# Graph attention on one core: GpSimd's two gathers of a pair also wait for VectorE's product of the pair four places back

## The chip, the cores and the metric

The kernel runs on one core of one Trainium2 chip. The metric is the device time of one execution in microseconds (us), of which the median of several executions counts. The engines are TensorE (PE; PEld is its weight load), VectorE (DVE), ScalarE (ACT), GpSimd (POOL) and SyncE (SP).

## The reference

One layer of graph attention with 8 heads, residual, a norm over the nodes and a norm over the features, all in fp32:

```python
Q, K, V = x @ Wq, x @ Wk, x @ Wv            # 6250 x 512, seen as 8 heads of 64
score = exp(clip(sum_d(K[src] * Q[dst]) / 8, -5, 5))      # 106250 edges x 8 heads
h = x + segment_sum(V[src] * score, dst) / (segment_sum(score, dst) + 1e-6)
h = (h - mean(h, 0)) * rsqrt(var(h, 0) + 1e-5) * gamma + beta
out = layernorm(x + h)                      # over the 512 features
```

The edges are sorted by `dst`.

## The kernel before

There are three stages. **project** (up to about 452 us of the profile) makes Q, K and V of 49 tiles of 128 nodes and stores K and V side by side in the HBM table `kv_d`, one row of 1024 fp32 numbers for each node. **attend** (about 452 to 1970 us) is the edge stage. **normalise** does the rest.

The edge stage works on 440 *pairs* of edge blocks; a block is up to 128 edges, one on each partition. A pair `q` has slot `s = q % 8` (`RING = 8`) of the buffer `kv`, which has 8 slots. Each engine has its own loop over the pairs, and `step(q, s, fills)` is one turn of it; `fills` counts how often the slot has been filled. What happens to pair q:

- GpSimd (`gather`, L747) issues two indirect DMAs of 128 rows x 4 KB each that fetch K and V rows of the edges' sources into `kv[:, s, u, 0:1024]`. They signal `s_g[s]`. `index` (L739) copies the row numbers of four pairs at a time.
- TensorE (L914) makes `q_ps`, the Q rows of the edges' destinations, from a one-hot matrix `mm_sb` and the Q rows of a node tile (`q_tile`). There is one `q_ps`: the step for pair q+1 waits until VectorE has used that of pair q (`s_mul`).
- VectorE multiplies K by `q_ps` in place (L794, *the product*, signals `s_mul[s]`), sums each head (L801), clips (L788).
- ScalarE takes the exponential (L855, signals `s_exp`) and weighs four heads of V with it (L841). VectorE weighs three heads (L710) and GpSimd one (L710, the same helper `weigh`). All three signal `s_v`.
- TensorE adds the weighed V rows to the node sums `acc` (L937, waits for `s_v`, signals `s_seg[s]`). It does so two steps behind, that is, after `q_ps` of the pair three on.
- GpSimd may gather the pair q+8 into the slot as soon as `s_seg[s]` says that pair q has been added up.

GpSimd's step is written in this order (`POOL_LAG = 5`): two gathers of pair q, at every fourth pair `index`, then the weighing of pair q-5. Its program has no other work in this stage. The engines' queues are worked in order, so whatever stands behind a wait waits too. SP loads a `q_tile` of 512 KB for each of the 49 node tiles.

`wait_apart(eng, sem, value)` waits for a semaphore's value; with a value in a register it makes the register, waits for 1 and then for the register's value. `at(s, fills, -4)` gives the slot and the count of the pair four back.

Of the kernel before, what the change touches and what calls it, by code (L numbers as in the profile page):

```python
# [44 lines left out]
RING = 8  # L45
# [29 lines left out]
def wait(eng, sem, value):  # L75

    if not (isinstance(value, int) and value <= 0):
        eng.wait_ge(sem, value)


def wait_apart(eng, sem, value):


    if not isinstance(value, int):
        value = eng.snap(eng.to_reg(value))
        eng.wait_ge(sem, 1)
    wait(eng, sem, value)
# [538 lines left out]
def attend(nc, block, kv_d, q_d, lb_d, nb_d, xb_d, tabs, agg, rz, kv, first, x_first, s_first, s_slots, soft):  # L626
    lb, nb, q_tile, zeros, less, eps = first
    src_t, bits_row, cnt_row, ident = tabs
    with ExitStack() as ctx:
# [9 lines left out]
        def sems(name):  # L639
            return [sem(f"{name}{s}") for s in range(RING)]  # L640
# [11 lines left out]
        s_mul, s_red, s_clip, s_exp = sems("s_mul"), sems("s_red"), sems("s_clip"), sems("s_exp")  # L652
# [6 lines left out]
        s_qx, s_evc, s_evict = (soft[n] for n in ("s_qx", "s_evc", "s_evict"))  # L659
        s_rz = soft["s_rz_early"]  # L660
        POOL_LAG = 5
        LOOKAHEAD, LAG = 3, 3

        def pipeline(eng, step, head):
# [9 lines left out]
        def there(q):  # L674
            return not isinstance(q, int) or 0 <= q < PAIRS

        def at(s, fills, ahead):

            return (s + ahead) % RING, fills + (s + ahead) // RING
# [26 lines left out]
        def weigh(eng, s, first, n):  # L706

            v = heads(kv[:, s, :, DIM:2 * DIM])[:, :, first:first + n, :]
            w = kv[:, s, :, 2 * DIM + first:2 * DIM + first + n].unsqueeze(3).broadcast_to([P, 2, n, D_HEAD])
            return eng.tensor_tensor(v, v, w, ALU.mult)  # L710

        @block.sync
        def _(sp):
            def load(t):
                sp.dma_start(q_tile[:, bass.ds(t % 2, 1), :].rearrange("p a n -> p (a n)"),
                             q_d[bass.ds(t * P, P), :]).then_inc(s_q, 16)

            sp.wait_ge(soft["s_tb"], 48)
            sp.wait_ge(soft["s_qa"], 16 * (TILES // 2 + 1))
            sp.wait_ge(soft["s_qb"], 16 * (TILES // 2))  # L720
            with sp.Fori(2, TILES) as t:
                used = sp.value_load(cnt_row[0:1, bass.ds(t - 2, 1)], min_val=1, max_val=VISITS)
                wait_apart(sp, s_qx, (used + 1) >> 1)
                sp.wait_ge(s_q, 16 * t)
                load(t)
            for t in range(FIRST_X):
                sp.dma_start(x_first[:, t, :], xb_d[t * P:(t + 1) * P, :]).then_inc(s_first, 16)
            for s in range(X_SLOTS):
                t = FIRST_X + 4 * s
                sp.wait_ge(s_seg[s], (PAIRS - 1 - s) // RING + 1)  # L730
                sp.dma_start(x_in_kv(kv, t, 4).rearrange("p (t n) -> p t n", n=DIM),
                             xb_d[t * P:(t + 4) * P, :].rearrange("(t p) n -> p t n", p=P)).then_inc(s_slots, 16)

        @block.gpsimd
        def _(pool):
            def index(q, s, fills):
                last = s + IDX_PAIRS - 1
                wait_apart(pool, s_g[last], 32 * (fills - 1))
                pool.tensor_copy(idx[:, s:last + 1, :].rearrange("p a n -> p (a n)"),  # L739
                                 src_t[:, bass.ds(2 * q, 2 * IDX_PAIRS)]).then_inc(s_idx[s // IDX_PAIRS], 1)  # L740

            def gather(q, s, fills, u):
                if u == 0:
                    if s % IDX_PAIRS == 0:
                        wait_apart(pool, s_idx[s // IDX_PAIRS], fills)
                    wait_apart(pool, s_seg[s], fills - 1)
                pool.indirect_dma_start(kv[:, s, u, 0:2 * DIM], None, kv_d,  # L747
                                        bass.IndirectOffsetOnAxis(idx[:, s, u:u + 1], 0),
                                        bounds_check=N_NODES - 1, oob_is_err=False
                                        ).then_inc(s_g[s], 16)  # L750

            def step(q, s, fills):
                p = q - POOL_LAG
                sp, fp = at(s, fills, -POOL_LAG)
                if there(q):
                    gather(q, s, fills, 0)
                    gather(q, s, fills, 1)
                if there(q + 2) and s % IDX_PAIRS == IDX_PAIRS - 2:
                    index(q + 2, *at(s, fills, 2))
                if there(p):  # L760
                    wait_apart(pool, s_exp[sp], fp)
                    weigh(pool, sp, HEADS - POOL_HEADS, POOL_HEADS).then_inc(s_v[sp], 1)
            pool.wait_ge(soft["s_trc"], 1)
            index(0, 0, 1)

            pool.wait_ge(soft["s_kva"], 16 * (TILES // 2 + 1))
            pool.wait_ge(soft["s_kvb"], 16 * (TILES // 2 + 1))
            for s in range(RING):
                step(s, s, 1)
            with nc.Fori(1, ROUNDS, engines=[pool.engine], head_slot={pool.engine: POOL_HEAD}) as i:  # L770
                for s in range(RING):
                    step(i * RING + s, s, i + 1)
            for q in range(ROUNDS * RING, PAIRS + POOL_LAG):
                step(q, q % RING, q // RING + 1)
# [531 lines left out]
def program(nc, xT, x, wq, wk, wv, gamma, beta, edges, dlast, out):  # L1306
# [7 lines left out]
    with ExitStack() as ctx:  # L1314
        def sb(name, shape, dt):
            return ctx.enter_context(nc.sbuf_tensor(name, shape, dt))


        soft = {name: ctx.enter_context(nc.semaphore(name)) for name in (
            "s_dl", "s_rows", "s_td", "s_tb", "s_lbd", "s_bet", *(f"s_xr{n}" for n in range(XB_RING)),  # L1320
            *(f"s_xbst{n}" for n in range(XB_RING)), *(f"s_g{n}" for n in range(RING)))}
        soft.update((name, ctx.enter_context(nc.semaphore(name))) for name in (
            "s_kva", "s_kvb", "s_qa", "s_qb", "s_q", "s_nb", "s_mem", "s_kc", "s_split", "s_visit", "s_trc", "s_xb",
            "s_qx", "s_evc", "s_evict", "s_rz_early", *(f"s_seg{n}" for n in range(RING)), *(f"s_lb{n}" for n in range(RING // LB_PAIRS))))
        tabs = (sb("src_t", [P, VCOLS], I32),
                sb("bits_row", [1, MASKS], I32),
                sb("cnt_row", [1, 64], I32),
                sb("ident", [P, P], F32))
        kv = sb("kv", [P, RING, 2, KVW], F32)
        first = (sb("lb", [P, RING, 2 * P], BF16),  # L1330
                 sb("nb", [P, P], BF16),
                 sb("q_tile", [P, 2, 2 * DIM], F32),
                 sb("zeros", [P, HALF // 2], BF16),
                 sb("less", [P, 1], F32),
                 sb("eps", [P, 1], F32))
        block = ctx.enter_context(nc.Block())
        project(nc, block, xT, x, wq, wk, wv, beta, edges, dlast, xb_d, kv_d, q_d, t_d, cnt_d, lb_d, nb_d, tabs, kv, first, soft)
        agg = sb("agg", [P, TILES, AGG], F32)
        rz = sb("rz", [P, TILES, HEADS], F32)
        x_first = sb("x_first", [P, FIRST_X, DIM], F32)  # L1340
        s_first, s_slots = (ctx.enter_context(nc.semaphore(name)) for name in ("s_first", "s_slots"))
        attend(nc, block, kv_d, q_d, lb_d, nb_d, xb_d, tabs, agg, rz, kv, first, x_first, s_first, s_slots, soft)
        normalise(nc, block, xb_d, gamma, out, tabs[-1], agg, rz, kv, first, x_first, s_first, s_slots, soft)
# [33 lines left out]
```

## Time and profile before

| what | us |
|---|---|
| median of the 3 runs shown | 2110.19 (2108.66 to 2122.17) |
| span of the profiled execution | 2119.3 |
| PE busy | 1935.2 |
| DVE busy | 1719.8 |
| ACT busy | 1377.4 |
| POOL busy | 1340.1 |

The profiled execution's own time is its span, 2119.3 us; it lies 9.1 us above the median and inside the three runs' spread. The busy times are of the whole span, which has stages with different limits; the edge stage is some 1518 us of it and is the only stage that the change touches. A matmul's end in the profile is modelled, so an engine that waits for a matmul can be seen to start a little after its shown end.

### The profile page before, as it was taken

To read this page: it belongs to the slowest core of one execution; us is meant where nothing else is said; L and a number is where in the kernel's file an instruction comes from. 1 tells how busy PE (TensorE), PEld (TensorE's weight loads), DVE (VectorE), ACT (ScalarE), POOL (GpSimd) and SP (SyncE) were. 2 spreads that over 40 slices of the span, in tenths; PEclk is the share of its full clock that TensorE was granted. 3 is DMA by queue.
4 is the path that set the end of the run, shared out by engine and by line. 5 is a ranking of instruction groups with operands and counts; after the bars stand their busy time and mean duration, and the time that the engine had idled before them with its cause. 6 is when DMAs were issued, how large, how long until landed. Compare 5 with 4: busy or idle time off the path is not lost.

```text
span 2119.3 us, 42713 instructions
## 1 busy us (share of the span) xinstructions
PE 1935.2 (91%) x7903; PEld 1358.3 (64%) x8014; DVE 1719.8 (81%) x2454; ACT 1377.4 (65%) x4602; POOL 1340.1 (63%) x1693
## 2 busy tenths in 40 slices
PE   8999999979989989898999999989999898998897
PEld 4555555537666767666666767767767676766433
DVE  6676655538888888888888888889888888888988
ACT  0011000017878878887878888878888887887866
POOL 0106663036777767777777777777777777676657
PEclk9999999999999999999999999999999999999999
DMA  4648886458888888888888889998899898889607
GB/s 172 176 154 301 298 289 233 145 225 273 299 309 302 309 304 303 301 313 310 301 300 320 310 304 315 324 312 305 314 324 318 291 319 314 281 316 320 225 0 288
DMA packets 184521, 589.09 MB, mean 278 GB/s; under 512 B 28480, under 2 KB 30240, under 8 KB 184480
## 3 DMA queue, kind: packets, MB, share of 16 engines
q0 software_dynamic: 135904, 465.14, 63.1%
q1 hardware_dynamic: 45120, 121.69, 16.3%
q10 hardware_dynamic: 3456, 1.78, 0.3%
q8 instruction: 18, 0.29, 0.1%
q14 instruction: 23, 0.19, 0.0%
HBM read 535.27 MB, written 78.91 MB: 290 GB/s over the span
## 4 chain that ended last, share of the span: by engine, by line
PE 67%; DVE 16%; issue 6%; ACT 4%; another core or an unknown queue 3%; DMA 2%; ACTq 1%; SPq 0%; POOL 0%; DVEq 0%
PE acc L937 21%; PE q_ps L914 21%; PE places L342 20%; DVE kv L794 8%; DVE raw L801 3%; ACT kv L841 2%; PE mm_ps L922 2%; DVE stats L1275 1%; DVE agg L1259 1%; DMA q_tile<-q_d 1%; PE places L402 1%; PE mm_ps L924 1%; ACT mm_sb L851 1%; DVE agg L1268 1%
## 5 line engine op out<-in xcount | busy, mean ns | idle before, releaser
L747 POOL DMA_INDIRECT kv<-kv_d,idx x880 | 898.3, 1021 | 505.4 <-issue 178.2
L841 ACT ACTIVATE kv<-kv 128x64 f32<-128x64 f32 x3520 | 888.8, 335 | 14.3
L937 PE MATMUL acc<-kv,mm_sb 128*128 128x260 f32 x3520 | 857.4, 387 | 6.6 <-ACT kv L841 0.6
L937 PEld LDWEIGHTS acc<-kv,mm_sb 128*128 128x128 f32 x3520 | 676.8, 193 | 111.4 <-issue 6.7
L794 DVE TENSOR_TENSOR kv<-q_ps,kv 128x1024 f32<-128x1024 f32 x440 | 537.6, 1222 | 183.4 <-PE q_ps L914 106.0
L914 PE MATMUL q_ps<-q_tile,mm_sb 128*128 x1760 | 546.5, 433 | 144.1 <-DVE kv L794 106.1
L801 DVE TENSOR_REDUCE raw<-kv 128x16 f32<-128x1024 f32 x440 | 532.8, 1211 | 0.0
L914 PEld LDWEIGHTS q_ps<-q_tile,mm_sb 128*128 128x128 f32 x1760 | 318.2, 190 | 290.1 <-issue 246.2
L851 ACT ACTIVATE mm_sb<-mm_ps,less 128x1024 fp32r<-128x1024 f32 x220 | 241.2, 1096 | 26.2 <-issue 13.6
L855 ACT ACTIVATE kv<-raw 128x16 f32<-128x16 f32 x440 | 92.4, 210 | 245.6 <-DVE raw L788 126.6
L710 DVE TENSOR_TENSOR kv<-kv 128x384 f32<-128x384 f32 x440 | 244.8, 556 | 4.0 <-ACT kv L855 2.9
L710 POOL TENSOR_TENSOR kv<-kv 128x128 f32<-128x128 f32 x440 | 181.0, 411 | 22.9 <-ACT kv L855 15.0
L342 PE MATMUL places<-t_sb,s_sb 128*128 128x512 f32 (+1 forms) x552 | 185.5, 486 | 0.0
L435 ACT COPY p<-places 128x768 f32<-128x768 f32 x23 | 18.4, 798 | 247.6 <-PE places L342 247.6
L342 PEld LDWEIGHTS places<-t_sb,s_sb 128*128 128x128 f32 x552 | 104.9, 190 | 73.6 <-issue 66.5
L342 PE MATMUL places<-w_sb,x_sb 128*128 128x512 f32 (+1 forms) x368 | 126.2, 486 | 0.0
L342 PEld LDWEIGHTS places<-w_sb,x_sb 128*128 128x128 f32 x368 | 69.8, 190 | 49.1 <-issue 44.5
L788 DVE TENSOR_SCALAR raw<-raw 128x16 f32<-128x16 f32 x440 | 85.8, 195 | 15.3
L922 PEld LDWEIGHTS mm_ps<-nb,lb 128*128 128x128 bf16 x880 | 51.4, 100 | 63.9 <-issue 63.9
L922 PE MATMUL mm_ps<-nb,lb 128*128 128x128 bf16 x880 | 90.0, 226 | 0.0
L590 DVE TENSOR_TENSOR u<-places,p 128x768 f32<-128x768 f32 x23 | 22.0, 958 | 79.6 <-PE places L342 79.6
L440 ACT COPY kv_a<-places 128x256 f32<-128x256 f32 x23 | 8.5, 371 | 100.0 <-PE places L342 60.2
(171 smaller groups left out, 1357.1 us busy)
## 6 DMA issues: line engine op xcount, KB each, us to landing
q_tile<-q_d SPq DMA_DIRECT2D x49, 512.0 KB
kv<-kv_d,idx POOLq DMA_INDIRECT x880
kv_d<-kv_a SPq DMA_DIRECT2D x25, 512.0 KB
xb<-in_x POOLq DMA_DIRECT2D x49, 256.0 KB, 4.1
xb_d<-xb POOLq DMA_DIRECT2D x49, 256.0 KB, 3.4
out_rows<-agg SPq DMA_DIRECT2D x49, 256.0 KB, 2.1
x_sb<-in_xT SPq DMA_DIRECT2D x24, 512.0 KB, 8.2
q_d<-q_a SPq DMA_DIRECT2D x24, 512.0 KB
```

The source lines that it names most:

```text
L342: last = pe.matmul(out[:, cols], left[:, c, :], right[:, c, cols], start=fresh and c == 0, stop=c == DEEP - 1, skip_group_check=True)
L710: return eng.tensor_tensor(v, v, w, ALU.mult)
L747: pool.indirect_dma_start(kv[:, s, u, 0:2 * DIM], None, kv_d, bass.IndirectOffsetOnAxis(idx[:, s, u:u + 1], 0), bounds_check=N_NODES - 1, ...
L788: dve.tensor_scalar(raw[:, s1, :, :], raw[:, s1, :, :], -5.0, 5.0, ALU.max, ALU.min).then_inc(s_clip[s1], 1)
L794: dve.tensor_tensor(k, q_ps[:, :, :], k, ALU.mult).then_inc(s_mul[s], 1)
L801: dve.tensor_reduce(raw[:, s, :, :], heads(kv[:, s, :, 0:DIM]), AX.X, ALU.add).then_inc(s_red[s], 1)
L841: return act.activation(v, v, ACT.Copy, scale=kv[:, s, u, 2 * DIM + h:2 * DIM + h + 1])
L851: act.activation(mm_sb[:, sa // 2, :, :], mm_ps[:, :, :], ACT.Relu, bias=less[:, 0:1]).then_inc(s_mm[sa // 2], 1)
L855: act.activation(kv[:, s, :, 2 * DIM:KVW], raw[:, s, :, :], ACT.Exp).then_inc(s_exp[s], 1)
L914: last = pe.matmul(q_ps[:, u, :], one_hot(sb_, u, 1), part_q, start=(n == 0), stop=(n == 1))
L922: pe.matmul(mm_ps[:, 0, n * P:(n + 1) * P], lb[:, sa + n // 2, n % 2 * P:(n % 2 + 1) * P], nb[:, :], start=True, stop=True)
L937: last = pe.matmul(acc[:, bass.ds(par, 1), DIM - (1 - n) * HALF:DIM + n * HALF], m, kv[:, sc, u, DIM + n * HALF:DIM + (n + 1) * HALF], sta ...
```

## The change

Before the first of the two gathers of pair q, GpSimd waits, besides for the slot (`s_seg`), until VectorE's product of pair q-4 is done. The first four pairs have no such wait.

```diff
         POOL_LAG = 5
+        GATHER_LAG = 4
         LOOKAHEAD, LAG = 3, 3
...
                     if s % IDX_PAIRS == 0:
                         wait_apart(pool, s_idx[s // IDX_PAIRS], fills)
                     wait_apart(pool, s_seg[s], fills - 1)
+                    if there(q - GATHER_LAG):
+                        wait_apart(pool, s_mul[(s - GATHER_LAG) % RING], at(s, fills, -GATHER_LAG)[1])
                 pool.indirect_dma_start(kv[:, s, u, 0:2 * DIM], None, kv_d,
```

No instruction changes its place. GpSimd's queue in the loop, three pairs of it (slots 0 to 2), is this before, with the semaphores that each entry waits for:

```order
L747 DMA kv<-kv_d,idx 128x1024 [waits s_idx0,s_seg0]
L747 DMA kv<-kv_d,idx 128x1024
L710 TENSOR_TENSOR kv<-kv 128x2x64 [waits s_exp3]
L747 DMA kv<-kv_d,idx 128x1024 [waits s_seg1]
L747 DMA kv<-kv_d,idx 128x1024
L710 TENSOR_TENSOR kv<-kv 128x2x64 [waits s_exp4]
```

and this with the change (all lines of this part of the file have moved down):

```order
L750 DMA kv<-kv_d,idx 128x1024 [waits s_idx0,s_seg0,s_mul4]
L750 DMA kv<-kv_d,idx 128x1024
L711 TENSOR_TENSOR kv<-kv 128x2x64 [waits s_exp3]
L750 DMA kv<-kv_d,idx 128x1024 [waits s_seg1,s_mul5]
L750 DMA kv<-kv_d,idx 128x1024
L711 TENSOR_TENSOR kv<-kv 128x2x64 [waits s_exp4]
```

The order is the same; each first gather has one more semaphore to wait for, and the weighing of the pair five back stands behind it.

## Rows read from the trace of the kernel before

**Rows 1.** Busy time (count) by stretch, the edge stage; then PEclk, DMA share, GB/s

```profile
452.00:1970.00 1518.00, 1367.84 (x6277) 1050.34 (x6386) 1311.46 (x1765) 1230.56 (x4267) 1096.66 (x1429) 0.98 0.88 309
```

**Rows 2.** Waits, 455 to 1970 us: us in total, times, longest

```profile
PE q_ps L914 <- DVE kv L794: 106.1, 117, 8.4
DVE kv L794 <- PE q_ps L914: 106.0, 148, 2.1
POOL kv L747 <- PE acc L937: 86.3, 63, 4.3
DVE kv L794 <- remote: 69.1, 27, 7.0
```

**Rows 3.** Timeline, GpSimd: start, us, what, idle before

```profile
1004.79 1.04 POOL L747 DMA_INDIRECT kv<-kv_d,idx  x1 [0.87 <-remote]
1006.14 1.00 POOL L747 DMA_INDIRECT kv<-kv_d,idx  x1 [0.31 <-issue]
1007.16 0.41 POOL L710 TENSOR_TENSOR kv<-kv 128x128 f32<-128x128 f32 x1
1007.73 1.03 POOL L747 DMA_INDIRECT kv<-kv_d,idx  x1 [0.16 <-issue]
```

**Rows 4.** Timeline, VectorE, the same stretch

```profile
1004.16 1.23 DVE L794 TENSOR_TENSOR kv<-q_ps,kv 128x1024 f32<-128x1024 f32 x1 [0.73 <-PE q_ps L914]
...
1007.10 1.22 DVE L794 TENSOR_TENSOR kv<-q_ps,kv 128x1024 f32<-128x1024 f32 x1
1008.23 0.55 DVE L710 TENSOR_TENSOR kv<-kv 128x384 f32<-128x384 f32 x1
...
1010.83 1.23 DVE L794 TENSOR_TENSOR kv<-q_ps,kv 128x1024 f32<-128x1024 f32 x1 [0.70 <-PE q_ps L914]
...
1017.52 1.22 DVE L794 TENSOR_TENSOR kv<-q_ps,kv 128x1024 f32<-128x1024 f32 x1 [0.74 <-PE q_ps L914]
```

**Rows 5.** Timeline, TensorE's sums of two pairs

```profile
1009.89 1.92 PE L937 MATMUL acc<-kv,mm_sb 128*128 128x260 f32 x8
...
1036.19 1.92 PE L937 MATMUL acc<-kv,mm_sb 128*128 128x260 f32 x8
```

**Rows 6.** Timeline, GpSimd, the gather that the second of those sums released

```profile
1038.95 1.02 POOL L747 DMA_INDIRECT kv<-kv_d,idx  x1 [1.45 <-PE acc L937]
```

**Rows 7.** The instructions of L747, who waited for them: us, times

```profile
  DVE kv L794: 1.7, 1
```

**Rows 8.** Timeline, GpSimd, the first pairs of the stage

```profile
461.29 0.99 POOL L747 DMA_INDIRECT kv<-kv_d,idx  x1 [0.30 <-issue]
462.58 1.00 POOL L747 DMA_INDIRECT kv<-kv_d,idx  x1 [0.30 <-issue]
...
470.64 0.19 POOL L739 COPY idx<-src_t 128x8 int32<-128x8 int32 x1 [0.20 <-DMA kv<-kv_d,idx]
```

**Rows 9.** Timeline, VectorE, products of pairs 0 and 2

```profile
462.00 1.23 DVE L794 TENSOR_TENSOR kv<-q_ps,kv 128x1024 f32<-128x1024 f32 x1 [1.75 <-issue]
...
475.04 1.23 DVE L794 TENSOR_TENSOR kv<-q_ps,kv 128x1024 f32<-128x1024 f32 x1 [7.05 <-remote]
```

**Rows 10.** Timeline, GpSimd, first gather of the last pair, 439

```profile
1955.84 1.04 POOL L747 DMA_INDIRECT kv<-kv_d,idx  x1 [0.85 <-remote]
```

**Rows 11.** Timeline, VectorE, product of pair 435

```profile
1955.20 1.23 DVE L794 TENSOR_TENSOR kv<-q_ps,kv 128x1024 f32<-128x1024 f32 x1 [0.72 <-PE q_ps L914]
```

**Rows 12.** Timeline, GpSimd, a weighing beside VectorE's

```profile
1037.09 0.40 POOL L710 TENSOR_TENSOR kv<-kv 128x128 f32<-128x128 f32 x1
```

**Rows 13.** Timeline, VectorE, a product that waited long, and a weighing

```profile
1033.14 1.23 DVE L794 TENSOR_TENSOR kv<-q_ps,kv 128x1024 f32<-128x1024 f32 x1 [2.91 <-remote]
...
1037.21 0.70 DVE L710 TENSOR_TENSOR kv<-kv 128x384 f32<-128x384 f32 x1
```

**Rows 14.** Timeline, GpSimd, around that long wait (pairs 163 and 167)

```profile
1018.16 1.04 POOL L747 DMA_INDIRECT kv<-kv_d,idx  x1 [0.87 <-remote]
...
1030.87 1.04 POOL L747 DMA_INDIRECT kv<-kv_d,idx  x1 [0.17 <-issue]
```

## The prediction

> **What bounds the kernel now.** I read the busy time of the edge stage first, then its waits, then the timelines of GpSimd and VectorE side by side; the last decide. The stage takes 1518 us, and no engine fills it: PE 1368, DVE 1311, ACT 1231, POOL 1097 us [rows 1]. It is a ring of two engines. The product (L794) needs `q_ps`, and TensorE may make the next `q_ps` only when the product is done: each waits for the other, 148 times and 106.0 us in one direction, 117 times and 106.1 us in the other [rows 2]. In the timeline the products start at 1004.16, 1007.10, 1010.83 and, two on, 1017.52 [rows 4]: 2.94 us where VectorE is busy throughout, 3.73 us where it idles 0.70 for `q_ps`, and 3.34 us a pair over four pairs. That pattern sets the time.
>
> GpSimd is not in that ring. A pair costs it 2.94 us (first gather at 1004.79, that of the next pair at 1007.73, nothing but 0.16 to 0.31 us of issue between) [rows 3], and it has 3.34. Its idle time is on the slot's release by TensorE's sum: 63 waits with 86.3 us [rows 2], and others that the profile calls remote. Only once did a product wait for a gather, 1.7 us [rows 7].
>
> **Does the new wait bind?** Pairs are numbered by counting both kinds of rows from the stage's start (880 gathers, 440 products). The gather at 1004.79 is of pair 159, and the product of pair 155, four back, runs from 1004.16 to 1005.39 [rows 3, 4]: the gather starts 0.60 us before its end. So it goes nearly everywhere: from pair 4 (462.58 against an end at 463.23 [rows 8, 9]) to pair 439 (1955.84 against 1956.43 [rows 10, 11]) the first gather starts before that product's end for 428 of 436 pairs, and for half of them by 0.5 to 0.6 us. It will bind nearly always.
>
> **How late the gathers become.** A released gather doesn't start at once: the sum shown from 1036.19 to 1038.11 released one that started at 1038.95, 0.84 us after [rows 5, 6]. So the first gather will start 0.84 us behind the product's end where it now starts 0.60 before it: 1.44 us later. Behind a long stall it is more: with the product of pair 163 late (start 1033.14, end 1034.37) GpSimd had gone ahead to pair 167 at 1030.87 [rows 13, 14]; now that gather starts at 1035.2, 4.3 us later. The pitch stays: GpSimd's 2.94 us a pair fits into the products' 2.94 to 3.73, so the lateness is one shift, not a sum over pairs.
>
> **What hides it: the product of the pair itself.** The gathers of pair 159 are issued by 1007.14 and its product starts at 1017.52, 10.4 us on [rows 3, 4]. After the change that is 10.4 - 1.44 = 8.9 us, and where four products follow each other without idle time it is 4 x 2.94 - 1.23 - 0.84 - 2.35 = 7.3 us (2.35 from the start of the first gather to the end of the second [rows 3]). Needed is the landing time. The rows show it once, and at its worst: pair 3's second gather is issued by 462.28 and the copy that waits for it starts at 470.64, so it landed within 8.4 us, as the last of eight gathers issued every 1.30 us from 452.00 on [rows 8]. Part of that is their queue: eight times 512 KB at the 309 GB/s that the stage moves in the mean [rows 1] take 13.6 us, to 465.6, which is 3.3 us behind 462.28. In the steady pattern two gathers come in 3.34 us, the DMA engines are 88% busy [rows 1], and no such queue stands. So I estimate a landing at 8.4 - 3.3 = 5.1 us; the ends are 0 and 8.4. Then 2.2 to 3.8 us are left, and the cost on the path is **0**; at 8.4 the pairs with 7.3 us would lose 1.1 us each, the others nothing. The Trainium skill ("DMA: Bandwidth & Descriptors", Anatomy of one DMA) gives about 2.0 us plus bytes over 436 GB/s for such a transfer, 3.2 us for 512 KB by my working from it. No row here shows a lone gather; by that the sum would be 0 as well.
>
> **What stands behind the wait on GpSimd.** The second gather (same shift, above); at every fourth pair the copy of row numbers, 0.19 us [rows 8], needed two pairs later; and the weighing of pair q-5 (L710), which TensorE's sum of that pair waits for. It ends 2.35 + 0.03 + 0.41 = 2.8 us behind the first gather's start [rows 3], so 0.84 + 2.8 = 3.6 us behind the product of q-4. TensorE wants it in its step q-3, behind `q_ps` of q-2. The sum at 1009.89 begins 1.57 us behind the end (1008.32) of the product of 156 [rows 4, 5]; that is the sum of pair 154, whose weighing is the one at 1007.16, done at 1007.57, 2.3 us ahead. After the change it is done at 1009.0 and still 0.9 us ahead; with the copy between, 0.7. Cost **0**, covered by that margin; without it TensorE and then the product would be late by the difference, for at most every pair.
>
> **Both weighings at once.** GpSimd's weighing now ends up where VectorE's own begins. For the example it will run from 1008.6 to 1009.0, VectorE's from 1008.23 to 1008.78 [rows 4]. Where they overlap today VectorE's takes 0.70 instead of 0.55 us [rows 12, 13]. This meets about half the pairs, those 2.94 us behind the one before; the other half come 3.73 us apart and miss. That is 220 x 0.15 = 33 us at most on VectorE. But in the pattern the next product there has an idle 0.70 in front [rows 4] that takes it up. I count only the pairs outside the pattern, some 40 of the 220, with a part of the overlap: 40 x 0.05 = **2 us**. The Trainium skill ("GPSIMD Engine Reference", Key points) says that GpSimd shares its SBUF interfaces with VectorE and that the two contend when a VectorE instruction has two inputs in SBUF. Here the trace agrees (0.70 against 0.55), and it is the rule that speaks against this change.
>
> **Start and end.** Gathers 0 to 3 are as before. Pair 6 waits for product 2, which ended at 476.27 [rows 9]; its gathers are then issued by 479.5, and product 6 starts no earlier than 4 x 2.94 - 1.23 = 10.5 us behind 476.27, at 486.8, 7.3 us after them. 0. The new wait's own instructions run on GpSimd's sequencer while a gather is executed: 0. At the stage's end the last gather goes out 1.4 us later and nothing waits for it but its product, as above.
>
> **Sum.** 0 + 0 + 2 + 0 = 2 us on the profiled execution's 2119.3. The forecast is made against the median, 9.1 us lower: 2110 + 2 = **2112 us**. A measurement of this kernel can tell about 1% from no change (the three runs lie 13.5 us apart); within it, 2089 to 2131.
>
> **Rivals.**
> *Gathers land too late (slower).* With four pairs of lookahead instead of up to eight, a late landing is no longer hidden. Each of the 49 node tiles brings a 512 KB `q_tile` load into the same DMA engines, which are 88% busy [rows 1]. It decides from the point where a landing takes over 7.3 to 8.9 us. If each load costs one pair its 1.4 us: 49 x 1.4 = 69 us, 2179; half of it, 2145. Against: one 1.7 us wait in 440 pairs now [rows 7], though every product had only 1.4 us more.
> *The weighings collide on the path (slower).* All 220 overlaps are exposed: 2110 + 33 = 2143 at most; half, 2127.
> *GpSimd's run-ahead did harm (faster).* 27 products waited 69.1 us for something called remote [rows 2]. If bursts of early gathers caused it, holding them back wins part: half is 35 us, 2075. Against: ahead of the 2.91 us wait the gathers ran in the plain pattern, one of them, at 1018.16, with no burst [rows 14]; the burst came after it. A smaller gain could come from a shift of phase between the engines alone, which these rows can't price.
> *The wait does nothing* would need the product to be done already; 428 of 436 say no.
>
> **How the numbers follow.** The forecast case has 0.59 (its own range 2095 to 2131), the wait that does nothing 0.02 at the same time. Late landings have 0.14, of which 0.12 over 1%; exposed collisions 0.08, of which 0.04; the gain 0.17, of which 0.15. So faster 0.15, within 1% 0.59 + 0.02 + 0.02 + 0.04 + 0.02 = 0.69, slower 0.16. The range reaches into the rivals on both sides until about 2 in 10 is left out: 2084 to 2140.
>
> **What would show it.** In the changed profile the gathers start some 0.8 us behind the product four back, and GpSimd's idle time before L747 is put down to VectorE. Products still follow at 2.94 and 3.7 us; waits of L794 for gathers stay a few us; VectorE's L710 grows from 0.55 to about 0.6 in the mean. I am wrong if L794 waits for gathers tens of times (first rival), if L710 grows and the 0.7 us idle doesn't shrink (second), or if the remote waits vanish (third).

## The result

| | median of the runs, us |
|---|---|
| the kernel before, measured beside it (4 runs) | 2116.18 (2108.66 to 2126.3) |
| the changed kernel (4 runs) | 2302.56 (2297.98 to 2307.19) |
| ratio | 1.0881, 95% interval 1.0845 to 1.0917 |

The change costs 186 us, 8.8%. The forecast was 2112 us with a range up to 2140.

All of it is in the edge stage. Its busy time by stretch, in the changed kernel (columns as in [rows 1]):

```profile
452.00:2157.00 1705.00, 1424.31 (x6285) 1095.23 (x6395) 1324.93 (x1766) 1232.70 (x4270) 1102.45 (x1430) 0.95 0.82 275
```

The stage grew from 1518 to 1705 us. VectorE and GpSimd have nearly the same busy time, the DMA engines are less busy (0.82 against 0.88), and the granted clock fell from 0.98 to 0.95 of full speed. PE's busy time grew by 56 us, most of it, by my estimate, by that clock (1368 x 0.98 / 0.95 = 1411), and the time in which TensorE does nothing by 131 (from 150 to 281). The waits in the changed kernel's edge stage (us in total, times, longest):

```profile
POOL kv L750 <- DVE kv L797: 383.2, 191, 2.5
...
PE q_ps L917 <- DVE kv L797: 252.5, 157, 2.4
DVE kv L797 <- remote: 228.3, 113, 2.8
...
DVE kv L797 <- PE q_ps L917: 106.6, 87, 2.1
```

The first row is the new wait. GpSimd sits in it, and that costs something only if others then wait for GpSimd. The second and the third are the loss. Against [rows 2], TensorE waits for the product 252.5 us instead of 106.1, and the product waits 228.3 us for something that the profile calls remote, instead of 69.1. No row says that a product waits for a gather. That alone would prove little, since the trace lacks many records of landings (see the experiments), but 337 of the 356 us that VectorE idles ahead of products end within 0.2 us behind a recorded signal of `q_ps`. VectorE's weighing is hardly longer (559 ns in the mean; 556 before), and TensorE's sum waits for GpSimd's weighing only 2.3 us in all.

What "remote" is shows in the three timelines of one long wait. TensorE:

```profile
1006.49 1.20 PE L917 MATMUL q_ps<-q_tile,mm_sb 128*128 x4
1007.53 0.40 PE L925 MATMUL mm_ps<-nb,lb 128*128 128x128 bf16 x4
1007.76 0.38 PE L927 MATMUL mm_ps<-lb,nb 128*128 128x512 bf16 x1
1007.98 1.92 PE L940 MATMUL acc<-kv,mm_sb 128*128 128x260 f32 x8
1011.63 1.19 PE L917 MATMUL q_ps<-q_tile,mm_sb 128*128 x4 [1.74 <-DVE kv L797]
```

VectorE and then GpSimd in the same stretch:

```profile
1004.96 1.22 DVE L797 TENSOR_TENSOR kv<-q_ps,kv 128x1024 f32<-128x1024 f32 x1
...
1007.81 0.25 DVE L791 TENSOR_SCALAR raw<-raw 128x16 f32<-128x16 f32 x1
1010.10 1.23 DVE L797 TENSOR_TENSOR kv<-q_ps,kv 128x1024 f32<-128x1024 f32 x1 [2.05 <-remote]
...
1007.05 1.02 POOL L750 DMA_INDIRECT kv<-kv_d,idx  x1 [0.16 <-issue]
1008.38 1.00 POOL L750 DMA_INDIRECT kv<-kv_d,idx  x1 [0.31 <-issue]
1009.40 0.41 POOL L711 TENSOR_TENSOR kv<-kv 128x128 f32<-128x128 f32 x1
```

`q_ps` is issued at 1006.49, and its last matmul should end at about 1007.69. VectorE is free at 1008.06 and starts the product at 1010.10. The trace also holds the times at which semaphores were updated, which the rows do not print. The one that this product waited for was updated at 1010.01, **2.3 us after the modelled end**. The next two groups signal right behind it, `mm_ps` at 1010.15 and the sum at 1010.24. Between the first and the last of these three signals lie 0.23 us, though the eight matmuls of the sum alone are 1.92 us of TensorE's work. So TensorE had gone on working; what came late, and bunched, was its word that it was done. In the same time VectorE's own signal (1007.78, for work that ended at 1007.77) was on time.

So it goes again and again: of the 431 distances between products from the ninth pair on, 185 are 2.9 to 3.0 us and 120 are 4.9 to 5.3, where before 114 were 3.6 to 3.9 and six 4.9 to 5.3. The mean is 3.86 us instead of 3.42. VectorE's idle time ahead of the products sums up to 356 us instead of 183, and the part of it ahead of products that started over 0.5 us behind the modelled end of their `q_ps` is 293 us instead of 155. That is 138 of the 186 us. VectorE's account also closes as a whole: its idle time ahead of products grew by 173 us and its busy time in the stage by 13 (1311 to 1325). What makes up the other 35 us of idle time I didn't separate.

### The profile page after: what moved, and what is told of

Read it like the earlier page. It is cut to its first block, busy times and chain, and to the rows that moved or that the text cites. A ratio compares the mean times of both kernels' runs of the same rounds, so it can differ in the third digit from the quotient of the medians.

```text
span 2305.4 us, 43578 instructions
## 1 busy us (share of the span) xinstructions
PE 1989.2 (86%) x7903; PEld 1400.8 (61%) x8014; DVE 1731.2 (75%) x2454; ACT 1380.3 (60%) x4602; POOL 1344.8 (58%) x1693
## 4 chain that ended last, share of the span: by engine, by line
PE 42%; DVE 37%; another core or an unknown queue 9%; issue 7%; ACT 1%; POOL 1%; DMA 1%; DVEq 0%; ACTq 0%; SPq 0%; POOLq 0%
PE places L342 18%; DVE kv L797 17%; DVE raw L804 13%; PE q_ps L917 10%; PE acc L940 10%; DVE kv L711 2%; DVE raw L791 2%; DVE stats L1278 1%; DVE agg L1262 1%; PE mm_ps L925 1%; PE places L402 1%; DVE agg L1271 1%; POOL agg L1101 1%; PE mm_ps L927 1%
## 5 line engine op out<-in xcount | busy, mean ns | idle before, releaser
L940 PE MATMUL acc<-kv,mm_sb 128*128 128x260 f32 x3520 | 903.8, 403 | 12.7 <-issue 5.3
L797 DVE TENSOR_TENSOR kv<-q_ps,kv 128x1024 f32<-128x1024 f32 x440 | 538.0, 1223 | 356.3 <-remote 228.3
L940 PEld LDWEIGHTS acc<-kv,mm_sb 128*128 128x128 f32 x3520 | 713.8, 203 | 128.5 <-issue 7.2
L917 PE MATMUL q_ps<-q_tile,mm_sb 128*128 x1760 | 551.2, 435 | 267.8 <-DVE kv L797 252.5
L711 POOL TENSOR_TENSOR kv<-kv 128x128 f32<-128x128 f32 x440 | 190.6, 433 | 16.3 <-ACT kv L858 8.7
L791 DVE TENSOR_SCALAR raw<-raw 128x16 f32<-128x16 f32 x440 | 105.8, 240 | 15.2
L925 PE MATMUL mm_ps<-nb,lb 128*128 128x128 bf16 x880 | 96.4, 237 | 0.8 <-issue 0.8
```

What stands on the lines that cost most here:

```text
L791: dve.tensor_scalar(raw[:, s1, :, :], raw[:, s1, :, :], -5.0, 5.0, ALU.max, ALU.min).then_inc(s_clip[s1], 1)
L797: dve.tensor_tensor(k, q_ps[:, :, :], k, ALU.mult).then_inc(s_mul[s], 1)
L917: last = pe.matmul(q_ps[:, u, :], one_hot(sb_, u, 1), part_q, start=(n == 0), stop=(n == 1))
L925: pe.matmul(mm_ps[:, 0, n * P:(n + 1) * P], lb[:, sa + n // 2, n % 2 * P:(n % 2 + 1) * P], nb[:, :], start=True, stop=True)
L940: last = pe.matmul(acc[:, bass.ds(par, 1), DIM - (1 - n) * HALF:DIM + n * HALF], m, kv[:, sc, u, DIM + n * HALF:DIM + (n + 1) * HALF], sta ...
```

## The experiments

Eighteen kernels ran, in five sets. **The sets stand at two levels**, and no number below can be read without that: the same unchanged kernel before took 2106 to 2130 us in the first measurement and in the first set, and 1956 to 1965 us in all four later sets, on three chips; one chip gave both, the first set at the high level and the second at the low one. I compare ratios only within a set.

What each kernel's trace says of late signals stands here once. Counted are TensorE's groups of matmuls in the edge stage that end in a signal (440 `q_ps`, 440 sums and 110 of `mm_ps`; 220 of `mm_ps` in `e15`). A signal is late when its recorded time is over 0.3 us behind the modelled end; of the others the median is 0.014 us behind it. At the high level the trace has no record of some signals; a count of late ones can only be one of the recorded ones. The recorded ones are split by when they were due: 0.5 to 3.0 us behind the start of a pair's first gather, or at another time. GpSimd's two gathers take 2.33 us from the first one's start to the second one's end. The bounds of that stretch were chosen after the counts had been seen.

| kernel, level | late, of those recorded | no record | late, due in the stretch | late, otherwise | us a pair |
|---|---|---|---|---|---|
| before, high | 371 of 803 | 187 | 360 of 595 | 11 of 208 | 3.42 |
| after, high | 420 of 837 | 153 | 413 of 748 | 7 of 89 | 3.86 |
| e4_second, high | 336 of 791 | 199 | 329 of 648 | 7 of 143 | 3.42 |
| e1_clip5, high | 215 of 631 | 359 | 140 of 454 | 75 of 177 | 3.30 |
| e3_weighfirst, high | 406 of 835 | 155 | 402 of 764 | 4 of 71 | 3.77 |
| e2_lag3, high | 0 of 950 | 40 | 0 of 392 | 0 of 558 | 4.82 |
| e9_before_again, low | 0 of 990 | 0 | 0 of 800 | 0 of 190 | 3.06 |
| e10_after_again, low | 0 of 990 | 0 | 0 of 828 | 0 of 162 | 3.09 |
| e15_clip4_wf_again, low | 0 of 1100 | 0 | 0 of 815 | 0 of 285 | 3.29 |

The missing records are not TensorE's alone. In the kernel before at the high level the trace has 7151 of the 14080 updates by landing gathers and 847 of the 1320 updates by VectorE's products, sums over a head and clips; at the low level (`e9_before_again`) it has 14066 and 1317. But where VectorE, ScalarE and GpSimd have a record, on semaphores that only one line of one engine updates, not one is over 0.3 us late in any of the nine traces of the table. Late signals are seen of TensorE alone.

### First set (before: 2115.49 us, high level)

Four kernels that move the gathers or what stands behind them. `e1_clip5` waits for the clip of the pair five back, which ends about where the product of four back starts; `e2_lag3` waits for the product three back; `e3_weighfirst` has the weighing ahead of the gathers; `e4_second` has the wait ahead of the second gather alone.

```diff
e1:  GATHER_LAG = 5
     wait_apart(pool, s_clip[(s - GATHER_LAG) % RING], at(s, fills, -GATHER_LAG)[1])
e2:  GATHER_LAG = 3
e3:  in step(): weigh(...) of pair q-5 written ahead of gather(q, s, fills, 0)
e4: -if there(q - GATHER_LAG):              # inside "if u == 0"
    +if u == 1 and there(q - GATHER_LAG):
```

> The gathers of pair q wait for VectorE's clip of pair q-5, which ends just before the product of q-4 starts: the wait still binds nearly always and still forbids running ahead, but the gathers start some 0.3 to 0.4 us before the product's end, as they do in the kernel before, not 0.84 us behind it. Theory A (the time goes by where in the cycle of product and q_ps the gathers fall): about the time before, 2105 to 2150. Theory B (what costs is that GpSimd can't run ahead any more, so that each hiccup is paid in full): near the changed kernel, 2270 to 2310.

> The changed kernel with the wait for the product three back: the gathers start at the same place of the cycle (0.84 us behind a product's end), one pair later. Theory A: the place is the same, so about 2300 (2280 to 2330), unless data come late as well. Theory C (gathers' data come too late for the product): some 3.5 us less lead for each pair, so far slower, above 2450, with VectorE's product waiting for gathers in the waits.

> The changed kernel with GpSimd's weighing of pair q-5 in front of the gathers of pair q, so that it no longer stands behind the new wait. Theory D (the late weighing is what costs: TensorE's sum waits for it, or the two weighings meet): back to 2105 to 2150. Theory A: the gathers stay where they are, so it stays at 2270 to 2310.

> Only the second gather of a pair waits for the product four back; the first goes as in the kernel before. The second then starts 0.84 us behind the product's end at the earliest, which is about where it starts anyway, so the wait costs little by itself. Theory A: near the time before, 2105 to 2160. Theory B: run-ahead is cut as in the changed kernel, so 2270 to 2310.

| kernel | us | ratio (interval) | first gather against the end of the product four back, median |
|---|---|---|---|
| e1_clip5 | 2064.54 | 0.9748 (0.9701 to 0.9795) | 0.12 us before |
| e2_lag3 | 2732.96 | 1.2911 (1.285 to 1.2973) | 5.4 us behind |
| e3_weighfirst | 2273.0 | 1.0771 (1.0699 to 1.0843) | 0.88 us behind |
| e4_second | 2131.52 | 1.006 (1.003 to 1.009) | 0.5 us before; only the second gather waits |

Moving the gathers by one microsecond takes the kernel from 8.8% slower than before (in the first measurement, beside a kernel before at the same level) to 2.5% faster. `e1_clip5` forbids GpSimd to run ahead much as the change does, so the lost running ahead is not the loss either. The weighing's place gives back about one of the 8.8 points, and the intervals all but touch, so GpSimd's late weighing was not the bulk of the loss. The waits of `e2_lag3` show what it is when that weighing does come too late:

```profile
POOL kv L750 <- DVE kv L797: 807.1, 225, 5.1
DVE kv L797 <- PE q_ps L917: 749.6, 227, 6.5
...
PE acc L940 <- POOL kv L711: 477.8, 224, 3.9
```

Here the sum of a pair waits for the weighing behind the wait, `q_ps` of the next waits behind the sum, and the product behind that: a closed ring. It has no late signal among 950 recorded ones although its set stood at the high level, where 40 have no record; its stage moves only 220 GB/s.

### Second set (before: 1958.62 us, low level)

`e5_lag3_wf` and `e6_clip4_wf` put the weighing first, so that the ring just shown can't close, and make the gathers later still (product three back; clip four back). `e7_after_small` and `e8_before_small` leave out three quarters of the gathered data from the ninth pair on, with as many descriptors: each row brings 256 of its 1024 numbers.

```diff
e5:  weigh first, GATHER_LAG = 3
e6:  weigh first, s_clip in place of s_mul
e7, e8:
-                pool.indirect_dma_start(kv[:, s, u, 0:2 * DIM], None, kv_d,
+                full = isinstance(q, int) and q < RING
+                n = 2 * DIM if full else 256
+                rows_d = kv_d if full else kv_d.rearrange("r (a n) -> (r a) n", n=n)
+                pool.indirect_dma_start(kv[:, s, u, 0:n], None, rows_d,
```

> The wait is for the product three back, and GpSimd's weighing of pair q-5 stands in front of the gathers, so TensorE's sum no longer waits behind them (that wait was 460 us in the run with lag 3 alone). Same place of the cycle as in the changed kernel, one pair (some 3.4 us) less lead for the gathers' data. Theory A (only the place in the cycle counts): 2260 to 2310. Theory C (the gathers' lead counts, whatever the trace calls the wait): over 2400.

> The weighing first, and the gathers wait for the clip of pair q-4, which ends just before the product of q-3 starts: the gathers start where they do in the run that waits for the clip of q-5 (2065 us), but one pair later in lead; they start 1.7 to 2.5 us later than in the changed kernel. Theory A: 2050 to 2130, faster than the changed kernel although its gathers are later. Theory C: slower than the changed kernel, over 2300.

> The changed kernel with a quarter of the gathered bytes: from the ninth pair on each gather moves 256 instead of 1024 numbers a row (rows of other addresses, the rest of the slot keeps old values), with as many descriptors. It leaves out most of the gathered data. If it is the data's traffic or its landing that makes q_ps or the product late: most of the 186 us go, 2050 to 2150. If it is GpSimd's issue or the wait in its queue: 2250 to 2310.

> The same quarter of the bytes in the kernel before. If traffic makes q_ps late there too, by 0.7 us in every second pair: 440 x 0.35 and the long waits go, 1930 to 2020. If not: within 1% of before, 2095 to 2135.

| kernel | us | ratio (interval) |
|---|---|---|
| e5_lag3_wf | 2078.77 | 1.0598 (1.0572 to 1.0624) |
| e6_clip4_wf | 2058.44 | 1.0512 (1.0495 to 1.053) |
| e7_after_small | 1975.32 | 1.0083 (1.0067 to 1.01) |
| e8_before_small | 1960.85 | 1.0007 (0.9998 to 1.0017) |

Without most of its data the changed kernel was only 0.8% slower. I first took this for proof that the load of gathered data made the loss. It was not: the set stood at the low level, where there was next to no loss to remove, as the next set showed.

### Third set (before: 1960.82 us, low level)

The kernel before, the changed kernel and `e1_clip5` again, as they are, and `e12_lag5`, the changed kernel with `GATHER_LAG = 5`.

> The kernel before, unchanged, to have its profile beside the others of this call. In the last call its median was 1959 us, in the three calls ahead of it 2110 to 2116, on the same chip; within a call its runs agree to about 1%. Theory E (there are two levels of the whole kernel, set by something outside its code that holds for a call or a load): its profile tells by TensorE's ends of q_ps. At the low level: q_ps never late, stage 1345 us. At the high one: late by 0.7 us in every second pair, stage 1505 us.

> The changed kernel, unchanged. Theory E: if the level is low and holds for it too, it comes to about the time of its copy with a quarter of the bytes, 1975 to 1990, 1% over the kernel before. Theory A (the place of the gathers makes q_ps late): 1.06 to 1.09 times the kernel before at either level.

> The kernel whose gathers wait for the clip of q-5, unchanged. At the high level its ratio was 0.975. At the low level there is no late q_ps to win back: 0.998 to 1.01. If it stays at 2060 us with the kernel before at 1959, the level is not common to the kernels of a call.

> The changed kernel with the wait for the product five back, which is done 2 to 3 us before the gather starts anyway: it binds only behind a hiccup, where it forbids running ahead by more than about one pair. Theory B (run-ahead is what matters): slower than before by 3% or more. Theory A: within 1% of before.

| kernel | us | ratio (interval) |
|---|---|---|
| e9_before_again | 1961.87 | 1.0 (0.9989 to 1.0011) |
| e10_after_again | 1975.62 | 1.0083 (1.0066 to 1.01) |
| e11_clip5_again | 1990.67 | 1.0158 (1.0139 to 1.0178) |
| e12_lag5 | 1964.77 | 1.0018 (1.0008 to 1.0028) |

At the low level the same change costs 0.8%, 15 us, and `e1_clip5`, which won 2.5% in the first set, loses 1.6%. The stretch of the edge stage, first of `e9_before_again`, then of `e10_after_again`:

```profile
452.00:1810.00 1358.00, 1331.36 (x6273) 1035.99 (x6382) 1309.50 (x1760) 1225.53 (x4260) 1112.32 (x1428) 1.00 0.95 344
```

```profile
452.00:1821.00 1369.00, 1333.08 (x6268) 1034.31 (x6377) 1314.16 (x1760) 1225.09 (x4258) 1114.50 (x1428) 1.00 0.94 341
```

TensorE is busy for 98 and 97% of the stage; at this level it sets the time, and the waits of the ring that I had read are nearly gone. `e12_lag5` costs 0.2% here; it was not run at the high level. Here are TensorE, VectorE and GpSimd in `e10_after_again`, with the gathers at the same place against `q_ps` as in the long wait above:

```profile
1003.08 1.20 PE L917 MATMUL q_ps<-q_tile,mm_sb 128*128 x4
...
1006.13 1.28 PE L917 MATMUL q_ps<-q_tile,mm_sb 128*128 x4
...
1004.49 1.22 DVE L797 TENSOR_TENSOR kv<-q_ps,kv 128x1024 f32<-128x1024 f32 x1
...
1007.52 1.22 DVE L797 TENSOR_TENSOR kv<-q_ps,kv 128x1024 f32<-128x1024 f32 x1
...
1003.65 1.02 POOL L750 DMA_INDIRECT kv<-kv_d,idx  x1 [0.16 <-issue]
1004.98 1.00 POOL L750 DMA_INDIRECT kv<-kv_d,idx  x1 [0.30 <-issue]
```

`q_ps` ends at 1004.28, 0.63 us behind the start of a first gather, and the product starts at 1004.49. In the first measurement it ended at 1007.69, 0.64 us behind the start of a first gather, and the product started at 1010.10. The order of the work is the same; what differs is the signal.

### Fourth set (before: 1959.72 us, low level)

Four kernels again as they were: the changed kernel, `e7_after_small`, `e6_clip4_wf` and `e5_lag3_wf`.

> The changed kernel as it is, a third time. It took 2302.6 us where the kernel before took 2116, and 1975.6 where the kernel before took 1961. Theory 1: the level (whatever sets it) is common to the kernels of a call, so this run gives one of these two pairs and nothing between: 2290 to 2315 with before at 2105 to 2130, or 1972 to 1980 with before at 1957 to 1963. Theory 2: each kernel has a level of its own in each call: then a cross is possible, 1975 beside a before of 2115, or 2300 beside 1960.

> The changed kernel in which, from the ninth pair on, each gathered row brings 256 of its 1024 numbers with the same count of descriptors (three quarters of the gathered data are left out). If the kernel before is at its high level here: theory 1, the late completion of TensorE's q_ps needs the load of the gathered data, says it is gone, with at most 15 late ones and 1972 to 1985 us; theory 2, it has nothing to do with the gathered bytes, says late ones in every second pair as in the changed kernel, over 150 of them, and 2200 to 2300 us. If the kernel before is at its low level, both say 1975 within 5 us and the run tells nothing new.

> The weighing first, and the gathers behind the clip of the pair four back, a second time. It took 2058.4 with 53 late completions beside a kernel before that stood at 1958.6. Theory 1: the lateness there was its own, by where its gathers fall in TensorE's and VectorE's cycle: 2050 to 2065 again if before is at 1957 to 1963. Theory 2: the lateness came from outside the kernel, at random for each kernel and call: another time, 1980 to 2000 without late completions or over 2080 with more of them.

> The weighing first, and the gathers behind the product of the pair three back, a second time. It took 2078.8 with 94 late completions beside a kernel before at 1958.6. Theory 1 (its own phase makes the lateness): 2070 to 2088 again if before is at 1957 to 1963. Theory 2 (from outside): another time, near 1990 without late completions, or over 2100 with more.

| kernel | us | ratio (interval) |
|---|---|---|
| e13_after_third | 1976.81 | 1.0087 (1.007 to 1.0104) |
| e14_after_small_again | 1978.43 | 1.0089 (1.0072 to 1.0106) |
| e15_clip4_wf_again | 2059.32 | 1.0497 (1.048 to 1.0515) |
| e16_lag3_wf_again | 2081.04 | 1.0612 (1.0581 to 1.0644) |

The level came out low, so the question put to `e14` (does the lateness of the high level need the gathered bytes?) got no answer. The other two came back within 3 us of their first times: their loss is their own. My expectations called it late completions of `q_ps`, and that was wrong: they counted products that started late, and the count of signals above finds none late in `e15`, nor does the same count in `e16`. Its waits name the cause:

```profile
DVE kv L797 <- DMA kv<-kv_d,idx: 79.7, 56, 3.3
...
PE q_ps L917 <- DVE kv L797: 74.1, 55, 3.1
```

The products there wait for the gathers to land. In `e16_lag3_wf_again` it is 96 waits with 100.0 us.

### Fifth set (before: 1961.75 us, low level)

`e17_clip4_wf_small` is `e15` with three quarters of the gathered data left out, as in `e7`; `e18_weighfirst_again` is `e3_weighfirst` again.

> The kernel of the weighing first and the gathers behind the clip of the pair four back (2058.4 and 2059.3 us, 53 and 55 late completions, beside a kernel before at 1959), now with three quarters of the gathered data left out from the ninth pair on (the same count of descriptors, 256 of 1024 numbers each). Theory 1, the late completions of q_ps come from the load or the late landing of the gathered data: at most 15 late completions are left and the time falls to 1965 to 2000 us. Theory 2, they come from the phase of GpSimd's work (its descriptors and its weighing) against TensorE's, whatever the bytes are: 40 to 70 late ones and 2045 to 2070 us.

> The changed kernel with the weighing in front of the gathers, a second time; it took 2273.0 beside a before of 2115.5, with 163 late completions. Theory 1, the kernel before's low level (1957 to 1963) is one without lateness for every kernel whose gathers start about 1 us behind the product or sooner: 1965 to 2000 us. Theory 2, weighing first makes lateness by itself at either level, as it did with the clip of four back: 2040 to 2100 us with 40 to 100 late completions. If before stands at 2105 to 2130, both say 2260 to 2285 again.

`e17_clip4_wf_small` took 1967.19 us, ratio 1.0027 (1.0016 to 1.0039): 94 of the 100 us of loss are gone with the bytes, which settles that it was the landing. `e18_weighfirst_again` took 1970.68 us, 1.0049 (1.0031 to 1.0066), where it had been 7.7% slower in the first set.

### What the experiments settle

**Shown.** The loss at the high level stands and falls with TensorE's late signals: 138 of the 186 us are idle time of VectorE ahead of products that had to wait for one, and in the sets in which no signal is late the same change costs 15 to 17 us. Four kernels ran at both levels, and for each the late signals give about the whole distance between its two times:

| kernel | time, high minus low, us | VectorE's idle time that ended with a late `q_ps` signal, high, us |
|---|---|---|
| before | 154 | 158 |
| after | 327 | 298 |
| e3_weighfirst | 302 | 282 |
| e1_clip5 | 74 | 84 |

How large it is depends on where the gathers stand: `e1_clip5` has them one microsecond earlier than the change and has 84 us of it, not 298. It is not late gathers, since 337 of the 356 us end with a `q_ps` signal; not the weighing's place, by `e3_weighfirst`; not the overlap of weighings, by the 559 ns. Late gathers are a second, separate price, which starts further on (`e15` to `e17`).

The clock follows the idle time: it is 1.00 in this stage where TensorE hardly waits (`e10_after_again`), 0.98 in the kernel before at the high level, 0.95 in the changed one and 0.86 in `e2_lag3`, in the order of TensorE's idle time. That order doesn't prove which comes first, and how much of the rest (186 - 138 us) the clock adds I didn't separate.

**Argued from the counts.** At the high level a recorded signal is late mostly if it falls due in the stretch from 0.5 to 3.0 us behind a first gather's start: 360 of 595 against 11 of 208 in the kernel before, 413 of 748 against 7 of 89 in the changed one. `e1_clip5` fits badly: 75 of its 177 other signals are late, and it has the most without a record. Late signals often arrive at a time that goes by the gathers and not by TensorE: 311 of the 371 in the kernel before and 285 of the 420 in the changed one come 2.7 to 3.3 us behind the first gather's start, which is 0.4 to 1.0 us behind the end of the second. So the new wait, which ties the gathers' start to 0.84 us behind a product, ties them to TensorE's next `q_ps` as well, issued 0.3 us behind the same product. In the changed kernel 299 recorded `q_ps` signals are due 0.5 to 0.9 us behind a first gather's start, as the one shown (0.64), and 117 of them are late, by 2.1 us in the median. The other 182 are on time, so the place alone doesn't decide. Before, the gathers stood about 1.4 us earlier; the `q_ps` of 1003.32 fell due 2.3 us behind the start of a first gather (1001.04 by the trace), near the end of the stretch, and came 0.7 us late.

**Open.** What sets the level of a set, and why a signal can be held at all. It is not the chip alone, and not TensorE's work. It isn't the gathers alone either, since the low level has as many and they are issued alike; `e2_lag3` hints that traffic matters too, but I could not run a kernel with less data at the high level. The gaps in the record of updates come and go with the level, and every time on record belongs to a run whose span and clock were recorded, so none tells whether recording has a part in it.

The 15 us that the change costs at the low level are accounted for in part. TensorE's sum waits there for GpSimd's weighing, which now stands behind the gathers, 12 times with 6.5 us in `e10_after_again` and not at all in `e9_before_again`; `e18_weighfirst_again`, which has the weighing first, has no such wait and costs 9 us instead of 15 to 17. VectorE's weighing grew from 558 to 594 ns in the mean, but its busy time in the stage by only 5 us (1309.50 to 1314.16), and in `e17_clip4_wf_small` the weighing took 605 ns and the loss was 5 us, so the longer weighings are at most a small part.

## Why the prediction was wrong

By its own steps:

- **The wait binds nearly always, and the gathers start 0.84 us behind the product**: right. In the changed trace none of the 436 first gathers starts ahead of the end of the product four back; 365 start 0.84 to 0.90 us behind it, the others 0.77 to 2.6.
- **The landing is hidden, 0 us**: right for the cost, and nearer to the edge than I said. The high level's trace has only 19 of a pair's 32 landing records in the mean, so its own figures (4.4 us in the median from the end of the second gather's issue, 4.8 us or more to spare in nine of ten pairs) may be too good. At the low level (`e10_after_again`), where they are complete, the landing took 5.1 us in the median, as I had estimated; one pair in ten has less than 0.8 us to spare, and 4 products wait 4.6 us in all. The rival of late landings needs a shorter lead; `e15` and `e16` have it, and lose 100 and 121 us.
- **The weighing behind the wait still comes in time, 0 us**: nearly right, 2.3 us of waits in all, and 6.5 us at the low level. How near the edge was is seen in `e2_lag3`: one pair less of lead and it costs 477.8 us of waits on TensorE.
- **Both weighings at once, 2 us**: right at the high level (559 against 556 ns, 1 us). At the low level the mean rose by 36 ns (558 to 594), but VectorE's busy time by only 5 us.
- **"The pitch stays", and the products go on at 2.94 and 3.73 us**: this is the step that failed. The products' mean distance went from 3.42 to 3.86 us, which over 431 distances is 190 us, about the whole loss. I took the 0.70 us in front of every second product as a fixed property of the ring of TensorE and VectorE. It was itself a late signal: the `q_ps` that the product at 1004.16 waited for [rows 4] had its last matmul end at 1003.32 by the trace and signalled at 1004.06. A gap that changes with where GpSimd's gathers stand was entered as a constant, and a change that moves GpSimd was then priced at nothing on it. Once the gathers were moved, the gap grew from 0.7 to about 2.0 us where it occurs (the products that started over 0.5 us behind the modelled end of `q_ps` are 168 instead of 152, but idle 293 us instead of 155).
- **The rivals**: the remark that a shift of phase between the engines can't be priced was the right place to look, but I gave it only the side on which the kernel gets faster. The run-ahead was to show itself by the remote waits going away; they grew from 69.1 to 228.3 us.
- **The range** took all of its slower side from landing and weighing, so nothing in it could reach 2302. At the low level the change would have cost 15 to 17 us where I forecast 2, which is within 1%; but that would have been luck in part, since TensorE, busy for 97% of the stage there, and not the ring sets the time.

What could have been seen in the trace of before: the product's wait was named TensorE, and TensorE's group had ended 0.7 us sooner. Beside the product at 1004.16 [rows 4] stand these rows, of TensorE and of GpSimd's first gather:

```profile
1002.05 1.28 PE L914 MATMUL q_ps<-q_tile,mm_sb 128*128 x4
...
1001.04 1.02 POOL L747 DMA_INDIRECT kv<-kv_d,idx  x1 [0.16 <-issue]
```

The `q_ps` ends at about 1003.32, and the product starts 0.84 us behind that, of which VectorE was idle for 0.73. Of these 0.84 us only 0.1 lie between the signal (1004.06) and the product's start. A wait that outlasts its releaser by much more than that is not that releaser's work.

## What to carry to other kernels

Compare the end of the work that a wait is put down to with the end of the wait. Where they are apart by much more than elsewhere in the same trace, the gap is not a constant: find what it moves with before moving anything near it, and widen the range on both sides. And before an experiment is read, look at what the unchanged kernel took in that very set: a kernel that "cures" a loss in a set where the loss is absent has shown nothing, as `e7_after_small` nearly did here.

## What the runs showed of the hardware

- One and the same kernel has two levels that last over a whole set of measurements: 2106 to 2130 us and 1956 to 1965 us, 8% apart, while the stage ahead of the edge stage takes the same time at both (the edge stage's first product starts 462 to 467 us into the profile in all of them). At the low level not one of 990 TensorE signals is over 0.3 us late in the kernel before; at the high level 371 of the 803 recorded ones are, and 187 have no record.
- At the high level TensorE's signals can come 0.7 to 2.3 us after the modelled end of the matmuls and bunched: three groups within 0.23 us, of which one alone has 1.92 us of work. No recorded signal of VectorE, ScalarE or GpSimd is late there.
- The trace's record of semaphore updates tells the levels apart: 7151 of 14080 landing updates of the gathers at the high one, 14066 at the low one, in the same kernel.
- The order of two variants can depend on the level: `e1_clip5` has 0.9748 of the time of before at the high one and 1.0158 at the low one. No variant here is better at both.
